# Expert products of a mixture-of-experts block with the weights as the stationary operand

## The reference

```
top_w, top_i = top_k(softmax(x @ router_w.T), 2)     # 8 experts, 2 for each token
combine = top_w / sum(top_w), scattered to (tokens, 8)
for e in range(8):
    gate = x @ ws[e, :512, :].T
    up   = x @ ws[e, 512:, :].T
    out += combine[:, e:e+1] * ((silu(gate) * up) @ w2s[e].T)
```

## Time and profile before

| | us |
|---|---|
| median of 3 runs (lowest, highest) | 513.27 (512.68, 515.3) |
| the profiled execution, its own time | 515.15 |
| its span | 513.3 |
| TensorE matmuls busy | 433.3 (84%) |
| VectorE busy | 334.8 (65%) |
| ScalarE busy | 313.9 (61%) |
| GpSimd busy | 244.5 (48%) |
| expert part, first gate matmul to last scatter | 283.83 to 489.31 |

### The profile page before, as it was taken

How to read it: one execution, slowest core, us unless ns; L and a number is a source line. 1 busy time by engine, 2 the same in 40 slices (tenths; PEclk the granted TensorE clock), 3 DMA queues, 4 the chain that set the end, 5 groups by cost and what they waited for, 6 DMA issues and landing times.

```text
span 513.3 us, 9836 instructions
## 1 busy us (share of the span) xinstructions
PE 433.3 (84%) x3058; PEld 264.0 (51%) x3058; DVE 334.8 (65%) x1184; ACT 313.9 (61%) x460; POOL 244.5 (48%) x332
## 2 busy tenths in 40 slices
PE   1999898999796999889973899999999999999700
PEld 0555444445453555445532567666666666666500
DVE  7156987876779887977698424577657666762234
ACT  0486549997866677665997167555535666653115
POOL 0063411123565487555825375644555665554322
PEclk9999969999999999979996799999999999999955
DMA  8368899822246214412321024333343333343254
GB/s 274 69 166 246 258 353 330 255 77 63 63 123 213 93 52 141 122 41 85 124 83 32 10 35 91 73 66 49 53 63 53 59 57 55 62 63 43 28 167 173
DMA packets 32978, 57.25 MB, mean 112 GB/s; under 512 B 5025, under 2 KB 23585, under 8 KB 31394
## 3 DMA queue, kind: packets, MB, share of 16 engines
q1 hardware_dynamic: 18306, 39.60, 24.6%
q0 software_dynamic: 7488, 10.27, 12.9%
q10 hardware_dynamic: 7136, 6.77, 4.2%
HBM read 38.64 MB, written 17.97 MB: 110 GB/s over the span
## 4 chain that ended last, share of the span: by engine, by line
PE 44%; DVE 23%; DMA 18%; issue 8%; ACT 6%; POOLq 1%; ACTq 0%; POOL 0%; SPq 0%; DVEq 0%
DMA sum_rows<-PT,IDXA 16%; PE PS L1587 9%; DVE PS L995 8%; PE PS L298 6%; PE PS L1614 5%; PE PS L1366 4%; PE PS L1405 4%; PE PS L1440 3%; PE PS L1387 2%; PE PS L305 2%; ACT PT L779 2%; DVE W L1132 2%; PE PS L1606 2%; PE PS L1459 1%; ACT W L817 1%
## 5 line engine op out<-in xcount | busy, mean ns | idle before, releaser
L995 DVE CUSTOM_DVE_ANT_0 PS<-PS,CB 128x512 f32<-128x512 f32 (+3 forms) x256 | 121.2, 516 | 35.2 <-PE PS L1366 33.9
L1587 PE MATMUL PS<-W,PT 128*128 x468 | 114.9, 382 | 4.0 <-issue 3.9
L779 ACT ACTIVATE PT<-PS 128x1024 f32<-128x1024 f32 x80 | 81.3, 1021 | 36.8 <-PE PS L1388 36.3
L730 POOL DMA_INDIRECT sum_rows<-PT,IDXA x39 | 62.1, 1593 | 57.6 <-DMA sum_rows<-PT,IDXA 21.4
L1366 PE MATMUL PS<-KQ 96*128 96x512 bf16 (+3 forms) x256 | 64.5, 316 | 13.1 <-DVE MX L995 11.9
L1587 PEld LDWEIGHTS PS<-W,PT 128*128 128x128 f16 x468 | 43.8, 98 | 43.2 <-issue 6.5
L1387 PE MATMUL PS<-KQ 104*128 104x512 bf16 (+3 forms) x256 | 60.8, 308 | 0.4 <-ACT PT L779 0.4
L714 POOL DMA_INDIRECT KQ<-x_rows,IDXA x39 | 40.0, 1027 | 30.4 <-DVE WS L1249 18.1
L1405 PE MATMUL PS<-PT,VA 128*32 128x256 f32 (+3 forms) x512 | 45.0, 446 | 4.7 <-ACT PT L779 4.7
L1388 PE MATMUL PS<-CB 128*128 128x128 bf16 x256 | 48.1, 223 | 0.0
L1366 PEld LDWEIGHTS PS<-KQ 96*128 96x128 bf16 x256 | 20.0, 100 | 46.3 <-DVE MX L995 33.4
(11 more groups left out here) (230 smaller groups left out, 891.4 us busy)
## 6 DMA issues: line engine op xcount, KB each, us to landing
W<-w1T SPq DMA_DIRECT2D x8, 1024.0 KB, 8.5
qk_parts<-W SPq DMA_DIRECT2D x32, 192.0 KB, 3.2
KQ<-qk_parts SPq DMA_DIRECT2D x32, 192.0 KB, 2.9
KQ<-qk_parts SPq DMA_DIRECT2D x64, 64.0 KB, 3.0
x_rows<-X1S ACTq DMA_DIRECT2D x4, 516.0 KB, 3.6
W<-xT SPq DMA_DIRECT2D x4, 512.0 KB, 6.7
KQ<-qk_parts SPq DMA_DIRECT2D x16, 128.0 KB, 3.0
sum_rows<-X ACTq DMA_DIRECT2D x4, 512.0 KB, 3.2
```

Of the source, the lines that this page charges most:

```text
L730: pool.indirect_dma_start(acc_dram, bass.IndirectOffsetOnAxis(ap=IDXA[:, j, 0:1], axis=0), YS[j % TRIO], None, compute_op=ALU.add).then_in ...
L779: act.activation(PT[n][:, :], STb[slot_of(k, n)].rearrange("p a n -> p (a n)"), ACT.Exp).then_inc(s["exp"], 1)
L995: last = dve.tensor_tensor_reduce(src, src, maskS[:, TT * P - w:], 1.0, LOW, ALU.add, ALU.max, MX[p][:, h, i:i + 1])
L1587: last = mm(dst, XGT[j % TRIO][:, x_part, k, :], w1h[:, bass.ds(at, UNIT)], start=(k == x_part == w_part == 0), stop=(k == KC - 1 and x_pa ...
```

## The change

Gate and up exchange their operands: a 128x128 piece of the weights is now stationary, and 128 tokens of `XGT` move. The product comes out with the hidden columns on the partitions and the tokens along the free axis, four pieces of 128 columns side by side in the same PSUM bank. That is the form that the down product needs, so all transposes of the hidden tile and their copies go. VectorE writes the product straight into `HT`, which now has two buffers. The f16 splitting of hidden tile and down weights goes altogether; every tile has the plain f32 down product, one tile late. The part pairs are the same three, 48 matmuls a tile instead of 12. Two waits are written anew: SiLU of tile j waits for VectorE's product of tile j-1, and the combine weight waits for the one before it. A scratch area at the end moves to another buffer.

```
@@ tensor
             def half(j, e, dst, n, done):
-                for k in range(KC):
-                    for x_part, w_part in ((0, 0), (0, 1), (1, 0)):
-                        at = (e + k * NX) * (4 * UNIT) + (2 * n + w_part) * UNIT
-                        last = mm(dst, XGT[j % TRIO][:, x_part, k, :], w1h[:, bass.ds(at, UNIT)], start=(k == x_part == w_part == 0), stop=(k == KC - 1 and x_part == 1))
+                for c in range(FF // P):
+                    for k in range(KC):
+                        for w_part, x_parts in ((0, (0, 1)), (1, (0,))):
+                            at = (e + k * NX) * (4 * UNIT) + (2 * n + w_part) * UNIT + c * P
+                            for x_part in x_parts:
+                                last = mm(dst[:, c * P:(c + 1) * P], w1h[:, bass.ds(at, P)], XGT[j % TRIO][:, x_part, k, :],
+                                          start=(k == x_part == w_part == 0), stop=(k == KC - 1 and w_part == 1))
                 last.then_inc(done, 1)
...
-            def hidden_T(j):
+            def down(j, e):
                 pe.wait_ge(f["h"], j + 1)
...
-                    last = mm(YP[:, 0:E], HT[:, k, :], W2[k][:, bass.ds(e * E, E)], start=(k == 0), stop=(k == FF // P - 1))
...
+                    last = mm(YP[:, 0:E], HT[j % 2][:, k * P:(k + 1) * P], W2[k][:, bass.ds(e * E, E)], start=(k == 0), stop=(k == FF // P - 1))
...
@@ scalar
             def silu(j):
                 act.wait_ge(f["g"], j + 1)
+                if j:
+                    act.wait_ge(f["h"], j)
                 act.activation(SIL, G, ACT.Silu, scale=CW[:, :]).then_inc(f["sil"], 1)
...
@@ vector
-            for j in range(SPLIT_FROM):
+            for j in range(NTILES):
                 combine_weight(j)
...
-                if j:
-                    dve.wait_ge(f["th"], j)
-                dve.scalar_tensor_tensor(HH, U, CW[:, :], SIL, ALU.mult, ALU.mult).then_inc(f["h"], 1)
+                if j >= 2:
+                    dve.wait_ge(f["yp"], j - 1)
+                dve.scalar_tensor_tensor(HT[j % 2], U, CW[:, :], SIL, ALU.mult, ALU.mult).then_inc(f["h"], 1)
...
-                dve.wait_ge(f["th"], j + 1)
-                if j:
-                    dve.wait_ge(f["yp"], j)
-                dve.tensor_copy(HT.rearrange("p k t -> p (k t)"), HP).then_inc(f["ht"], 1)
```

More of the change, by code:

```diff
@@ L127, in block_kernel @@
         WLO = sb("WLO", [P, UNIT])
[L128 to L133, removed]
         F2 = [sb(f"F2{n}", [P, 1]) for n in range(2)]
@@ L211, in block_kernel @@
         XGT = [PT[1][:, 256 * n:256 * n + 256].bitcast(F16).rearrange("p (r k t) -> p r k t", r=2, k=KC) for n in range(3)]
-        SIL, HH = PT[2][:, 0:512], PT[2][:, 512:1024]
-        HT = PT[3][:, 0:512].rearrange("p (k t) -> p k t", k=4)
+        SIL = PT[2][:, 0:512]
+        HT = [PT[3][:, 512 * n:512 * n + 512] for n in range(2)]
         YS = [PT[4][:, 256 * n:256 * n + 256] for n in range(3)]
[L215 to L220, removed]
         IDXA = sb("IDXA", [P, NTILES, 1 + TOPK], I32)
@@ L264, in block_kernel @@
         s_xb, s_x1w, s_rows, s_w = sem("s_xb"), sem("s_x1w"), sem("s_rows"), sem("s_w")
[L266 removed]
+        f = {n: sem("c_" + n) for n in ("xt", "xgt", "g", "u", "sil", "h", "yp", "ys", "ws")}
         s_g = [sem(f"s_xg{q}") for q in range(TRIO)]
         s_acc = sem("s_acc")
[L269 removed]
+        G, U, XP, YP = bank[0], bank[1], bank[2], bank[4]
         XPh = XP.bitcast(F16)
[L271 removed]
         def nth(j):
@@ L931, in _ @@
                 ao_columns(B - 1, h, TB[h])
-            for j in range(SPLIT_FROM):
-                columns(j + 1)
+            for j in range(NTILES):
+                if j + 1 < NTILES:
+                    columns(j + 1)
                 silu(j)
@@ L946, in _ @@
                     store_rows(B - 1)
[L947 to L975, removed]
             result(NTILES - 1)
@@ L1248, in combine_weight @@
                 dve.wait_ge(s_g[j % TRIO], nth(j))
+                if j:
+                    dve.wait_ge(f["ws"], j)
                 dve.tensor_tensor_reduce(WT[:, :], XGW[j % TRIO], PICK[:, j, 1:1 + TOPK], 1.0, 0.0, ALU.mult, ALU.add, WS[:, j:j + 1]).then_inc(f["ws"], 1)
[L1251 to L1267, removed]
[L1268 to L1288 removed]
+            for j in range(NTILES):
                 combine_weight(j)
@@ L1599, in up @@
                 half(j, e, U, 1, f["u"])
-            def hidden_T(j):
+            def down(j, e):
                 pe.wait_ge(f["h"], j + 1)
-                if j:
-                    pe.wait_ge(f["ht"], j)
-                for k in range(FF // P):
-                    last = nc.tensor.transpose(HP[:, k * P:(k + 1) * P], HH[:, k * P:(k + 1) * P], ident)
-                last.then_inc(f["th"], 1)
-            def down(j, e):
-                pe.wait_ge(f["ht"], j + 1)
                 if j:
@@ L1670, in _ @@
             e_before = None
-            for j in range(SPLIT_FROM):
+            for j in range(NTILES):
+                if j == NEARLY:
+                    pe.wait_ge(s["tab"], 2)
                 e = expert(j)
                 gate(j, e)
-                rows_T(j + 1)
+                if j + 1 < NTILES:
+                    rows_T(j + 1)
                 if j == 0:
@@ L1693, in _ @@
                     mm(MISC[:, 0:NX], onesb, MRUN[:, :], start=True, stop=True).then_inc(s["cnt"], 1)
[L1694 to L1727 removed]
+                e_before = e
+            down(NTILES - 1, e_before)
         d = {n: sem("d_" + n) for n in ("stat", "var", "ve", "rs", "nm", "out")}
```

162 lines of the change are left out of this document (3 added, 159 removed).

## The result

The changed kernel takes 541.14 us (median of four runs, 540.45 to 543.27), the kernel before 513.14 beside it: a ratio of 1.0544, with a 95% interval of 1.0502 to 1.0586. The forecast was 532.5 with a range of 511 to 551, slower. The sign and the mechanism came out as forecast, and the forecast was 8.6 us too low. The profiled execution took 541.08 us, its span is 539.2.

What follows compares the result with a forecast made beforehand. It took TensorE's sequencer, executing register instructions, to bound the changed kernel: 38 rounds of 5.53 us from 289.8, plus other work and the end, put the last scatter at 508.3, 19.0 later; on 513.3 that gave 532.5 us, range 511 to 551.

Steps and rivals of the forecast that it cites:

- Array time: TensorE's array in the expert part: 48 matmuls 2.64, row transposes 0.22, down 1.73, together 4.59 us a tile.
- Register instructions block what stands behind them: TensorE's sequencer: a register instruction, taken as 0.11 us, holds up even later loads that need no register.
- Gate and up, 32 x 0.11 + 96 x 0.0075 = 4.24: Sequencer time of both products: 32 register instructions at 0.11 and 96 pushes at 0.0075, 4.24 us a tile.
- Reading the expert's number: Sequencer time to read the tile's expert number, taken from a stretch of the earlier trace: 0.68 us a tile.
- Down, 0.47: Sequencer time of the down product: one fused instruction, three single operations, 16 pushes; 0.38 to 0.56, taken as 0.47 us.
- Row transposes and separate waits: Sequencer time for 8 pushes and two or three waits a tile: 0.06 to 0.2, taken as 0.14 us.
- lead: How far the sequencer runs ahead during the two output projections: between 0 and 4.1 us, taken as 2.5.
- other work: Sequencer's work of tiles 3 to 8 (x1, logits, ranks, slots): between 0 and 3.5 us, taken as 1.5.
- Work said to be hidden: Array at 4.59 and scatter chain at 4.6 us a tile both hide behind the sequencer's 5.53.
- The first, that register work hides: Rival for the expert part: register work hides, array and scatter chain bind; 502.2 us, chance 0.13.
- The second, 0.096 us in a long row: Rival on the sequencer: a register instruction costs 0.096 instead of 0.11 us, no change, about 513; chance 0.09.
- The third: Rival on the array: loads of the new form don't overlap, tile 6.75 us, time 579; chance 0.05.

Runs made afterwards that it cites:

- e1: The changed kernel with gate and up weight addresses fixed at expert 0, so these 48 matmuls a tile need no register instruction: 505.29 us.
- e5: The changed kernel with byte weight addresses, four gate and up addresses computed in each fused register instruction (11 fused, 3 single a tile): 504.66 us.
- e7: The changed kernel with the expert's number read from the table a second time in each tile, between gate and up: 567.64 us.
- e8: The changed kernel with the down product's weights always those of expert 0, one fused and three single register instructions fewer a tile: 526.31 us.
- e10: The changed kernel with four more already fulfilled waits a tile in gate and up, two of them instructions of their own: 550.85 us.
- e3: The changed kernel with some second-matmul addresses worked out anew instead of reused, 8 more fused register instructions a tile: 582.46 us.

## Why the prediction was right, and where it fell short

- **Array time, 4.59 a tile.** Measured 4.69 (e1, e5): gate and up 1.34 each against 1.32, row transposes 0.23 against 0.22, down 1.78 against 1.73. Nearly right, and hidden in the changed kernel, as said.
- **Register instructions block what stands behind them.** Right, and it decides the case (e1, e5). The loads of XGT in the earlier trace rows, held up by an instruction that they don't need, were the right evidence. The Trainium skill, "Advanced Engine Details and Errata", section "Sequencer Loop", has other instructions queued while a control instruction runs; by that rule e1 and e5 would have changed nothing, and they gave 36 us. The measurement decides against it for this engine and these instructions.
- **Gate and up, 32 x 0.11 + 96 x 0.0075 = 4.24.** Measured 4.23. The agreement is luck in part: the instruction was too cheap (0.11 for 0.124), the pushes too dear (0.0075 each for next to nothing), and the longer intervals, which add 0.27 a tile to 32 x 0.124, weren't foreseen.
- **Reading the expert's number, 0.68.** Measured 0.70 (e7), 0.67 in the packed trace. The agreement is luck in part: the stretch of the earlier trace rows from which 0.68 was read holds a separate wait as well (it starts at 326.88 there, 0.11 before the next instruction). Read and wait together are 0.77 in the changed kernel, so the term was short by 0.1 of what it was read from.
- **Down, 0.47, of which 0.35 for its four register instructions.** Measured 0.50 with its pushes, and 0.39 to 0.44 for the four (e8): slightly short.
- **Row transposes and separate waits, 0.14.** This is the term that was mis-sized. The tile has three separate waits; with the row transposes they measure 0.35, and e10 gives 0.11 to 0.13 for each wait added. The prediction left 0.08 for them beside the pushes. I priced a wait at next to nothing because it is fulfilled, and it costs nearly a register instruction's time all the same.
- **The sum.** 0.67 + 4.23 + 0.35 + 0.50 is the measured tile, 5.74 with the unrounded terms, so nothing is left over. The tile was 0.21 longer than forecast, all of it from the separate waits, and that is 8.0 us in 38. The last scatter came 7.2 late, so lead, other work and the end together were taken 0.8 us too dear. The prediction's upper bounds of the terms add up to 6.0 and not to its 5.9; the measured tile is inside either.
- **From the last scatter to the time.** The 7.2 us make 539.7; the rest, 1.4, is that the forecast took off 1.9 us for a profiled run before that was slower than its median, while the profiled run of the changed kernel lies at its median.
- **Work said to be hidden.** Right. From 290 us to the last scatter TensorE waits for another engine once, and one scatter for the one before it (the view of waits of the changed kernel: us in total, times, longest):

```profile
POOL sum_rows L701 <- ACT PT L865: 101.0, 37, 4.2
...
POOL sum_rows L701 <- DMA sum_rows<-PT,IDXA: 2.8, 1, 2.8
...
PE PS L1453 <- ACT PT L865: 0.8, 1, 0.8
```

From 290 to 500 us the granted clock was 1.00, its upper level, as between 290 and 490 before.
- **Rivals.** The first, that register work hides, gave 502.2 us, and a last scatter at 478.2. It did not happen, but e5 is that kernel: 504.66 us, last scatter at 478.4. The second, 0.096 us in a long row, falls by e3 and by the starts in the packed trace, 0.124 in the row. The third falls by e1.

## What to carry to other kernels

An address that is worked out at run time costs TensorE's sequencer some 0.12 us, two matmuls of 128 columns. Before large matmuls are cut into small ones, count the sequencer's instructions for each of them, and put several addresses into one fused instruction, ahead of the matmuls that use them. Where a busy engine looks full but its consumers all wait for it, compare two products of the same kind: if the one behind long work is fast and the next is slow, the queue is dry. The gaps between single loads then show what writes it.

## What was not expected of the hardware

- The price of a sequencer instruction hangs little on what it does: 0.125 us for a fused one of three operations, about 0.11 for a single one, 0.11 to 0.13 for a separate wait that is already fulfilled. The comparison right behind the load of the expert's number takes longer, 0.21. A wait that rides on the next instruction cost nothing that shows, and an operation more inside a fused one at most some 0.006.
- Four additions fused into one instruction instead of four instructions turned 527.41 us into 504.66.
- A matmul with its load costs the sequencer so little beside this that 0.25 us for two register instructions and three pairs, and 0.125 for one and one, leave next to nothing for it.
